# The last block's end run tile by tile instead of stage by stage

## The reference

```python
x = x + attention(layernorm(x), ctx)        # its last addition belongs to the change too
n = layernorm(x)                            # over 512 features
q = n @ Wq.T                                # 16 router features
scores = q @ keys.T                         # 64 experts
gate = softmax over the 16 highest scores, 0 elsewhere
z = (n @ A.T).reshape(64, 8) * gate[:, None]
x = x + (z.reshape(512) @ B.T) * 2
```

## Time and profile before

| what | us |
|---|---|
| median of 3 runs (lowest, highest) | 2380.31 (2375.63, 2382.03) |
| profiled execution, device time | 2375.59 |
| its span, as the profile shows it | 2373.8 |
| PE busy in the span | 2096.9 (88%) |
| DVE busy | 1799.3 (76%) |
| ACT busy | 1057.8 (45%) |
| POOL busy | 587.2 (25%) |
| mean granted TensorE clock | 0.946 of full |

### The profile page before, as it was taken

The page is one execution under the profiler, slowest core; times in us unless marked ns, Lnnn a source line. Parts: engine busy times, 40 slices in busy tenths (PEclk is TensorE's granted clock), DMA queues, the critical chain, the costliest instruction groups (busy, mean ns, idle before and its releaser), DMA issues.

```text
span 2373.8 us, 27142 instructions
## 1 busy us (share of the span) xinstructions
PE 2096.9 (88%) x8248; PEld 1187.8 (50%) x8248; DVE 1799.3 (76%) x1804; ACT 1057.8 (45%) x2612; POOL 587.2 (25%) x405
## 2 busy tenths in 40 slices
PE   6877888989999979999999988998999889799987
PEld 2332453445555534445555544445555544577763
DVE  3599994389999985269999996359999994455543
ACT  2544441465565522265555532266555540233331
POOL 0099991001111110001111111001111111466630
PEclk9788999899999989989999999989999999799998
DMA  1468893138888871227888872226888773322210
GB/s 63 171 150 196 214 212 125 58 126 181 178 189 178 180 177 62 73 106 161 183 178 185 181 171 78 87 100 155 177 172 183 172 156 114 126 74 98 89 45 18
DMA packets 110073, 328.98 MB, mean 139 GB/s; under 512 B 12944, under 2 KB 13072, under 8 KB 107568
## 3 DMA queue, kind: packets, MB, share of 16 engines
q0 software_dynamic: 35328, 127.94, 29.0%
q1 hardware_dynamic: 68912, 189.58, 26.8%
q10 hardware_dynamic: 5760, 10.49, 1.2%
HBM read 183.00 MB, written 14.94 MB: 83 GB/s over the span
## 4 chain that ended last, share of the span: by engine, by line
DVE 39%; PE 30%; issue 17%; DMA 7%; ACT 4%; DVEq 1%; SPq 1%; POOL 1%; POOLq 0%; ACTq 0%; PEldq 0%
DVE hs L1132 13%; DMA xc<-hs 5%; PE acc L1444 5%; DVE hs L1139 5%; DVE hs L1304 4%; PE acc L1566 3%; DVE hs L1123 3%; PE pq L1497 2%; DVE qr L1169 2%; PE acc L1577 2%; PE acc L1656 2%; PE pq L1733 2%; PE pq L1527 2%; PE pk L1733 2%; DVE sc L1189 2%
## 5 line engine op out<-in xcount | busy, mean ns | idle before, releaser
L709 POOL DMA_DIRECT2D xc<-hs x192 | 165.8, 866 | 1306.9 <-DVE hs L1139 1270.9
L1132 DVE TENSOR_TENSOR_SCAN hs<-dA,hs 128x1024 f32<-128x1024 f32 x192 | 428.7, 2274 | 0.0
L892 ACT ACTIVATE dA<-dt,aneg 128x504 f32<-128x504 f32 x384 | 253.5, 707 | 254.3 <-DVE hs L1132 254.0
L1497 PE MATMUL pq<-qT,wa 128*128 128x512 f32 x768 | 354.7, 616 | 8.4 <-DVE sc L1189 8.4
L1577 PE MATMUL acc<-wb,oT 128*128 128x512 f32 x768 | 354.8, 607 | 3.6 <-ACT oT L880 3.6
L1139 DVE TENSOR_TENSOR hs<-hs,bc 128x1024 f32<-128x1024 f32 x256 | 307.6, 1203 | 2.2
L857 ACT ACTIVATE pr<-sc,mx 128x64 f32<-128x64 f32 x512 | 170.8, 335 | 243.1 <-DVE mx L1195 243.1
L1444 PE MATMUL acc<-xnT,wa 128*128 128x512 f32 x512 | 230.6, 604 | 10.4 <-PE acc L1444 4.4
L1497 PEld LDWEIGHTS pq<-qT,wa 128*128 128x128 f32 x768 | 146.9, 196 | 183.0 <-issue 172.8
L1123 DVE TENSOR_TENSOR hs<-u,bc 128x1024 f32<-128x1024 f32 x192 | 226.3, 1217 | 12.0 <-POOLq L702 6.0
L1577 PEld LDWEIGHTS acc<-wb,oT 128*128 128x128 f32 x768 | 142.3, 195 | 149.6 <-issue 145.5
(11 more groups left out here) (200 smaller groups left out, 3358.8 us busy)
## 6 DMA issues: line engine op xcount, KB each, us to landing
xc<-hs POOLq DMA_DIRECT2D x240, 512.0 KB, 7.0
bc<-bc_rows SPq DMA_DIRECT2D x64, 512.0 KB, 7.5
wa<-in_wq SPq DMA_DIRECT2D x64, 512.0 KB, 9.8
wb<-in_wo SPq DMA_DIRECT2D x64, 512.0 KB, 5.5
wa<-in_wx SPq DMA_DIRECT2D x16, 512.0 KB, 4.6
wa<-in_wz SPq DMA_DIRECT2D x16, 512.0 KB, 6.1
wb<-in_ow SPq DMA_DIRECT2D x16, 512.0 KB, 6.9
k<-k_rows SPq DMA_DIRECT2D x32, 256.0 KB, 11.0
```

The lines of the kernel that those rows point to most:

```text
L709: G.dma_start(xc[:, 2 * c:2 * c + 2, :], hs[:, c, :].rearrange("p (d t) -> p d t", t=T), accum_op=ALU.add).then_inc(s_y[c], 16)
L892: ins = S.activation(to[:, :, 1:SEQ], dt[:, s, :].rearrange("p (b t) -> p b t", t=SEQ)[:, :, 1:SEQ], ACT.Exp, scale=aneg[:, s, bass.ds(jj ...
L1132: V.tensor_tensor_scan(out=hs[:, c, :], data0=dA[:, c % 2, :], data1=hs[:, c, :], initial=0.0, op0=ALU.mult, op1=ALU.add).then_inc(scd.sem, 1)
L1497: ins = M.matmul(pq[:, h, :], wa4(p)[:, k, h * P:(h + 1) * P], qT[:, k, :], start=(k == 0), stop=(k == KE - 1))
```

## The change

In the last iteration alone, everything behind the output projection goes tile by tile. The last `project_o` signals each tile (`otd`). VectorE runs `begin(t)` (addition, bn_stats, bn_aggr, small addition) and `normed(t)` in the order begin 0, begin 1, normed 0, begin 2, normed 1 and so on, GpSimd one single-column pow for each tile. TensorE turns one tile (four transposes into one bank of `pk`), then per tile: router q (128 columns), A into `acc[:, t, :]`, the scores, and the turn of tile t + 2. ScalarE copies per tile. The gate is made per tile; the negated maximum is written before the second replacement. After A of all tiles, `turn_z`, B into `acc` and the last addition go by tiles, and SP stores each tile (256 KB) by itself. The other iterations are unchanged.

```diff
@@ sync
-                if attn:
+                if not mamba:
+                    for t in range(TT):
+                        eng.wait_ge(outr.sem, outr.upto(blk, t))
+                        eng.dma_start(out[blk][:, t, :], xn[:, t, :]).then_inc(s_out, 16)
+                elif attn:
@@ gpsimd
-                if attn:
+                if not mamba:
+                    for t in range(TT):
+                        eng.wait_ge(ln3.sem, ln3.upto(i - 1, t))
+                        G.tensor_tensor(rs[:, t:t + 1], ve[:, t:t + 1], mhalf[:, t:t + 1], ALU.pow).then_inc(ln3r.sem, 1)
+                elif attn:
                     rstd(i - 1, ln3, ln3r, TT)
@@ scalar: tail(), in place of evacuate and the rest
+                    copy_tile(x3T, ln3t, x3r, 0)
+                    copy_tile(x3T, ln3t, x3r, 1)
+                    for t in range(TT):
+                        route_q(t)
+                        if t + 2 < TT:
+                            copy_tile(x3T, ln3t, x3r, t + 2)
+                        gate_exp(t)
+                    for t in range(TT):
+                        copy_tile(zgT, zgt, zgr, t)
@@ vector: tail()
+                    def begin(t):
+                        eng.wait_ge(otd.sem, otd.upto(0, t))
+                        V.tensor_tensor(xa[:, t, :], xa[:, t, :], acc[:, t, :], ALU.add).then_inc(x2r.sem, 1)
+                        eng.wait_ge(x2r.sem, x2r.upto(blk, t))
+                        ct(V.bn_stats(stats[:, t, :], xa[:, t, :]))
+                        ct.wait()
+                        hold(eng)
+                        ct(V.bn_aggr(mv[:, t, :], stats[:, t, :]))
+                        ct.wait()
+                        V.tensor_scalar(ve[:, t:t + 1], mv[:, t, 1:2], LN_EPS, None, ALU.add).then_inc(ln3.sem, 1)
...
+                    for t in range(TT + 1):
+                        if t < TT:
+                            begin(t)
+                        if t >= 1:
+                            normed(t - 1)
+                    for t in range(TT):
+                        top_k(t)
+                        gated(t)
+                    for t in range(TT):
+                        eng.wait_ge(bwd.sem, bwd.upto(blk, t))
+                        V.tensor_tensor(xn[:, t, :], xa[:, t, :], acc[:, t, :], ALU.add).then_inc(outr.sem, 1)
@@ tensor: tail(), and otd in project_o
+                            if stop:
+                                ins.then_inc(otd.sem, 1)
...
+                    def route_scores(t):
+                        eng.wait_ge(rqr.sem, rqr.upto(blk, t))
+                        if t >= 1:
+                            eng.wait_ge(rex.sem, rex.upto(blk, t - 1))
+                        M.matmul(pq[:, 1, t * EXPERTS:(t + 1) * EXPERTS], k2T[0:RD, t * P:(t + 1) * P], rkw[:, :],
+                                 start=True, stop=True).then_inc(rsd.sem, 1)
...
+                    turn_x3(0)
+                    turn_x3(1)
+                    for t in range(TT):
+                        route_q(t)
+                        project_a(t)
+                        route_scores(t)
+                        if t + 2 < TT:
+                            turn_x3(t + 2)
+                    turn_z(0)
+                    for t in range(TT):
+                        if t + 1 < TT:
+                            turn_z(t + 1)
+                        project_b(t)
```

More of the change, by code:

```diff
@@ L307, in build @@
         rop = stage("rotary_ready", 1)
-        ac0 = stage("acc_cleared", 1)
+        otd = stage("tail_o_done", TT)
         qd = stage("q_done", PAIRS)
@@ L641, in _ @@
             iterations(eng, one)
-            eng.wait_ge(s_out, 16 * NBLK + LEAD)
+            eng.wait_ge(s_out, 16 * (NBLK - 1 + TT) + LEAD)
         @block.gpsimd
@@ L1011, in one, with tail, copy_tile, route_q @@
                         decays_and_units(n)
+                def tail():
+                    def copy_tile(to, done, ready, t):
+                        eng.wait_ge(done.sem, done.upto(blk, t))
+                        S.activation(to[:, :, t * P:(t + 1) * P], pk[:, t % 2, :].rearrange("p (k r) -> p k r", r=P),
+                                     ACT.Copy).then_inc(ready.sem, 1)
+                    def route_q(t):
+                        eng.wait_ge(rqd.sem, rqd.upto(blk, t))
+                        S.activation(k2T[0:RD, t * P:(t + 1) * P], pq[0:RD, 0, t * P:(t + 1) * P],
+                                     ACT.Copy).then_inc(rqr.sem, 1)
+                    def gate_exp(t):
+                        eng.wait_ge(rmd.sem, rmd.upto(blk, t))
+                        S.activation(gex[:, t, :], pq[:, 1, t * EXPERTS:(t + 1) * EXPERTS], ACT.Exp,
+                                     bias=negm[:, t:t + 1]).then_inc(rex.sem, 1)
+                    copy_tile(x3T, ln3t, x3r, 0)
[7 more added lines that the diff above has]
+                        copy_tile(zgT, zgt, zgr, t)
+                if not mamba:
+                    tail()
+                    return
                 if attn:
@@ L1344, in one, with tail, normed, top_k @@
                     cp.end()
+                def tail():
+                    ct = Chain(eng, ch_a, blk)
+                    def begin(t):
[8 more added lines that the diff above has]
+                        V.tensor_scalar(ve[:, t:t + 1], mv[:, t, 1:2], LN_EPS, None, ALU.add).then_inc(ln3.sem, 1)
+                    def normed(t):
+                        eng.wait_ge(ln3r.sem, ln3r.upto(blk, t))
+                        V.tensor_scalar(xn[:, t, :], xa[:, t, :], mv[:, t, 0:1], rs[:, t:t + 1], ALU.subtract,
+                                        ALU.mult).then_inc(ln3n.sem, 1)
+                    def top_k(t):
+                        eng.wait_ge(rsd.sem, rsd.upto(blk, t))
+                        hold(eng)
+                        raw = pq[:, 1, t * EXPERTS:(t + 1) * EXPERTS]
+                        ct(V.max(top[:, t, 0:8], raw))
+                        ct.wait()
+                        hold(eng)
+                        ct(V.match_replace(rsc[:, t, :], top[:, t, 0:8], raw, NEG))
+                        ct.wait()
+                        hold(eng)
+                        ct(V.max(top[:, t, 8:16], rsc[:, t, :]))
+                        V.tensor_scalar(negm[:, t:t + 1], top[:, t, 0:1], -1.0, None, ALU.mult).then_inc(rmd.sem, 1)
+                        ct.wait()
+                        hold(eng)
+                        ct(V.match_replace(rsc[:, t, :], top[:, t, 8:16], rsc[:, t, :], NEG))
+                        ct.wait()
+                    def gated(t):
+                        eng.wait_ge(rex.sem, rex.upto(blk, t))
+                        ct(V.scalar_tensor_tensor(out=gate[:, t, :], in0=rsc[:, t, :], scalar=NEG, in1=gex[:, t, :],
+                                                  op0=ALU.is_equal, op1=ALU.mult))
+                        ct.wait()
+                        ct(V.tensor_reduce(gs[:, t:t + 1], gate[:, t, :], AX.X, ALU.add))
+                        ct.wait()
+                        ct(V.reciprocal(gs[:, t:t + 1], gs[:, t:t + 1]))
+                        ct.wait()
+                        ct(V.tensor_scalar(gate[:, t, :], gate[:, t, :], gs[:, t:t + 1], SCALING, ALU.mult, ALU.mult))
+                        ct.wait()
+                        eng.wait_ge(awd.sem, awd.upto(blk, t))
+                        V.tensor_tensor(zg[:, t, :].rearrange("p (e r) -> p e r", r=RANK),
+                                        acc[:, t, :].rearrange("p (e r) -> p e r", r=RANK),
+                                        gate[:, t, :].unsqueeze(2).to_broadcast([P, EXPERTS, RANK]),
+                                        ALU.mult).then_inc(zgd.sem, 1)
+                    eng.wait_ge(s_xa, blk * 16 + 16)
+                    eng.wait_ge(s_out, 16 * blk + LEAD)
+                    for t in range(TT + 1):
[9 more added lines that the diff above has]
+                        V.tensor_tensor(xn[:, t, :], xa[:, t, :], acc[:, t, :], ALU.add).then_inc(outr.sem, 1)
@@ L1417, in _ @@
         def _(eng):
-            lead(eng, ln1t, inx, ssd, ssg, dtd, rot, ac0, qd, vd, sd, ptd, pvd, wod, ln3t, rqd, rsd, awd, zgt,
+            lead(eng, ln1t, inx, ssd, ssg, dtd, rot, otd, qd, vd, sd, ptd, pvd, wod, ln3t, rqd, rsd, awd, zgt,
                  bwd, inz, opd, ln2t, wad, wbd)
@@ L1568, in project_o @@
                                                    stop=(stop and h == 1 and n == 2))
-                        if half == 1:
+                            if stop:
+                                ins.then_inc(otd.sem, 1)
+                        if half == 1 and not stop:
                             ins.then_inc(wod.sem, 1)
@@ L1738, in one, with tail, turn_x3, route_q @@
                             eng.drain().then_inc(wbd, 1)
+                def tail():
+                    def turn_x3(t):
+                        eng.wait_ge(ln3n.sem, ln3n.upto(blk, t))
+                        if t >= 2:
+                            eng.wait_ge(x3r.sem, x3r.upto(blk, t - 2))
+                        for k in range(KE):
```

(40 more changed lines are left out.)

## The result

The changed kernel takes 2363.4 us as a median of 8 runs (2358.7 to 2370.0), the kernel before 2375.7 in the 8 runs beside it: 12.3 us less, ratio 0.9951 with a 95% interval of 0.9937 to 0.9964. Timed a second time, the ratio was 0.9960 (0.9945 to 0.9974). The range of 2362 to 2376 held the median, close to its lower end.

What follows compares the result with a forecast made beforehand. Behind the last output projection, engines work strictly in turn with nothing to hide it. Savings of 9.9 (start), 1.0 (selection) and 1.8 (store), against 0.7 and 1.5 (clock), give 10.8 less: 2380.3 to 2369.5, put at 2369; range 2362 to 2376.

Steps and rivals of the forecast that it cites:

- B: Second large matmul group by tiles, with the turns of tiles 2 and 3 inside: 15.1 us against 14.4, 0.7 more.
- tail: End of the last projection matmul to the end of the span: 56.1 us before, forecast 10.8 less.
- The start: Normalising by tile from the projection's end until the router starts: 3.5 us instead of 13.4, 9.9 less before the clock.
- Router and A: Router and first large matmul group by tile, VectorE's selection for tiles 0 to 2 hidden: 19.4 us against 19.7.
- The clock: TensorE falls to half speed after the sparse stretch ahead of the router, costing 1.5 us, by the first return seen.
- The alternative of full clock: Rival: turns break the idle stretch and the 1.5 us are not paid; 12.3 us less, 2368; chance 0.16.
- half clock in all of A: Rival: router and A stay at half clock, each matmul group waiting for VectorE or ScalarE; 2387 at 17 us more; chance 0.04.
- the two returns: Full clock returning 3.0 or 5.1 us after work resumed, costing 1.5 or 2.6 us; the first was taken.
- From A to B: Selection of tile 3 and ScalarE's z copy ahead of B's first tile: about 2.2 us against 3.2, 1.0 less.
- The store: Four stores of 256 KB instead of one of 1024 KB at the end: 1.8 us saved, bounds 1.5 and 2.1.
- The third rival: Turns wait for VectorE's queue, tile 1 turned no earlier than tile 3 is normalised; 6.2 us less, 2374; chance 0.19.

Runs made afterwards that it cites:

- shapes: Changed kernel with full-size operands in the router's two products, so its gates differ: 4.94 us a tile against 5.55, tail 44.1 us.
- waits: Changed kernel with scores of tile t - 1 behind router q of tile t, their waits gathered ahead: 5.41 us a tile, tail 45.9 us.
- keep_clock: Changed kernel with 14 more transposes into an unused bank between the turns of tiles 0 and 1: tail 44.5 us against 46.1.
- norm_only: Only the first half: normalisation, router, A and gate by tile; z turn, B, additions and single store as before: tail 54.1 us against 56.1 before.
- z_early: Changed kernel with turn and copy of z of tile 0 ahead of router q and A of tile 3: tail 44.9 us against 46.1.
- end_only: Only the second half: z turn, B, additions and stores by tile, the rest as in the kernel before: tail 54.4 us against 56.1.

## Why the prediction was right, step by step

| step | predicted us | measured us |
|---|---|---|
| projection to router | 3.5 | 3.2 |
| router and A, clock left out | 19.4 | 21.1 |
| the clock | 1.5 | 1.6 |
| scores(3) to B | 2.2 | 2.1 |
| B | 15.1 | 14.9 |
| last addition and store | 3.6 | 3.2 |
| tail | 45.3 | 46.1 |

- **The start** is as worked out: the first turn lies 0.35 us behind the projection and the second 2.65, where 0.4 and 2.9 were forecast. GpSimd's pow on one column took 0.58 to 0.80 us instead of the 1.0 I took, but for tiles 0 to 2 VectorE came to the normalised piece later anyway.
- **Router and A** is the term that was mis-sized, by 1.7 us. I priced the small pieces at their pitch and gave nothing for going from one to the next. The 22.7 measured (2322.69 to 2345.42) less the 1.6 of the clock are 21.1, and 19.4 were forecast. Four times the steps of a tile give A 14.5 instead of 13.9, router q 3.9 instead of 3.4 and the scores 1.5 instead of 1.0; the two turns take 1.2 instead of 0.9. By shapes and waits this is 13 changes of operand shape in four tiles at about 0.14, or 1.8. That they cost this was shown; what the array does in that time was not.
- **The clock** fell as taken and cost 1.6 by keep_clock. The alternative of full clock did not occur, and neither did half clock in all of A: VectorE's piece per tile (3.2 to 3.5 from the first max to the end of the multiply) stayed under TensorE's 5.55. Half clock lasted 3.4 us. Which of the two returns seen in before (3.0 or 5.1 us) would hold was a choice and not worked out. The rule of the Trainium skill on bursts (TensorE: Matmul & The Clock Gate, "HAM oscillation — how this bites in real kernels") is about work that is followed by a wait each time. The trace agrees in norm_only's gap before B, where TensorE stood for 3.0 us and the clock fell; in the change TensorE never stands between router(0) and scores(3), and the clock fell once, which cost 1.6 us.
- **From A to B**: the idle 1.1 us (about 1.5 were forecast) was released by ScalarE's copy, as expected. z_early shows that no data forces it.
- **The store** saved 2.2 instead of 1.8.

The third rival, a router held until VectorE has normalised all tiles, did not happen: router(0) started at 2322.69, while the last normed piece started at 2324.79. The mechanism was right, and part of the closeness of the numbers is luck. In the tail the 1.7 too little for router and A is half made up by 0.9 too much in the start, from A to B, in B and in the store. The forecast median of 2369 was 5.6 too high chiefly because the three runs of before that were shown had a median 4.6 above that of the eight. The difference was forecast as 10.8 and measured as 12.3, with 8.6 to 15.0 as its interval; the tails say 10.0. The lower end of the range, which the median came near, stood there for a clock that stays up, and it did not stay up.

## What to carry to other kernels

When a stage-by-stage end is cut into tiles, look for the last tile's chain that a stage used to hide: it must find cover in the next stage, or the cut gives back much of what it won, as the first half alone did. After the cut, read the strict orders again: three exchanges of instructions that depend on nothing between them gave another 4.4 us. And a gap on TensorE is worth more than its length when the clock falls in it or just behind it: 2.2 us more in norm_only's B.

## What the runs showed of the hardware

- Going between matmuls of 128x128 operands and ones of 16 rows or 16 columns cost 0.14 to 0.15 us each time on average at full clock (5.55, 5.41 and 4.94 us a tile with four, three and no changes). The step from the scores to the next piece took 0.37 us with a semaphore wait and 0.36 without.
- The clock depends on more than the gap: the same 8.3 us of idling left TensorE at half speed for 5.1 us from the start of its work before and for 8.8 us in end_only (2325.1 to 2334.0), a difference of 1.8 us in the time of the same code.
- Of the some 10 us between executions most lies ahead of the tail: the last projection matmul ended between 2310.2 and 2320.8 in the thirteen profiles, while the changed kernel's tail repeated to 0.1 us in two of them. The 1.8 us of the clock after the old gap is the part found in a tail.
